# A frequency-mixing kernel: the last group of four takes other PSUM banks, and the edge columns are merged later

## The chip, the cores and the metric

The kernel runs on one core of a Trainium2 chip. The metric is the device time of one execution in microseconds (us), lower is better. The engines that matter are TensorE (PE in the profile; PEld is its weight load), VectorE (DVE), ScalarE (ACT), GpSimd (POOL) and SyncE (SP, which issues the large DMAs). Each has its own queue of instructions, works through it in order, and waits for the others by semaphores. PSUM, into which TensorE writes, has eight banks of 512 float32 for each of 128 partitions.

## The reference, cut to what matters

The input x is (4, 128, 128, 768) float32. The 768 channels are 8 blocks of 96, and each block has its own complex two-layer mixing.

```python
xf = jnp.fft.rfft2(x, axes=(1, 2), norm='ortho')            # (b, h, 65, c), then c -> 8 x 96
o1r = relu(einsum(xr, w1[0]) - einsum(xi, w1[1]) + b1[0])
o1i = relu(einsum(xi, w1[0]) + einsum(xr, w1[1]) + b1[1])
o2r = einsum(o1r, w2[0]) - einsum(o1i, w2[1]) + b2[0]
o2i = einsum(o1i, w2[0]) + einsum(o1r, w2[1]) + b2[1]
xc = softshrink(o2r, 0.01) + 1j * softshrink(o2i, 0.01)
return jnp.fft.irfft2(xc, s=(128, 128), axes=(1, 2), norm='ortho') + x
```

## The kernel before, in words

All transforms are matrix products with tables of cosines and sines. The work is cut into 32 steps (L23: `STEPS = B * NB // PAIRS` = 16 turns of a loop with two steps each), one for each pair of an image and a block of 96 channels. A step `q` has these stages.

1. Forward transform along one axis (`forward_lines`, L367): 26 groups of up to four channels. DVE or ACT packs each into `ring_a`, PE multiplies, and ACT or DVE moves the result from PSUM into `ydg`, an array of 128 columns (real and imaginary parts of the 65 frequencies kw) by 96 channels.
2. Mixing: the frequencies kw are worked through in 17 groups (`NU`; `GROUP_PAIRS`, L63), numbered u = 0 to 16. Groups 0 to 15 have four kw each, group 16 has one, kw = 1. Group 1 holds the edge columns kw = 0 and 64, and group 15 holds kw = 2 to 5. For each group PE does the transform along H (`fwd_big` L407, `fwd_small` L420), whose results are copied out of PSUM by ACT (`copy_big`, L567, into `zbig`) and DVE (`copy_small`, L668, into `zsmall`); PE does the first mixing layer (`mix1_whole`, `mix1_columns`, `mix1_rows`), ACT applies the relu (`relu`, L574: first `hsmall`, then `hbig`), PE does the second layer (`mix2_rows`, `mix2_whole`), and DVE adds the bias and applies the soft threshold (`shrink`, L675: three instructions of which the first, L691, reads PSUM, and the last, L701, writes `ydg`).
3. `merge` (L482) combines the edge columns by two matmuls, and ACT copies the result into columns 0 and 1 of `ydg` (L610).
4. Inverse transform along H (`inverse_lines`, L390): again 26 groups of up to four channels. The first six are packed into the ring `ring_h` in two parts: ACT takes columns 12 to 127 (L614), which need groups 0 to 14 of the mixing alone, and DVE takes columns 0 to 11 (L745), which need all groups and the merge. PE starts a group when both parts are there.
5. Inverse transform along W (`rows`, L488), with DVE and POOL adding the results onto the input, and SP storing them.

The order is written out by hand. PE's mixing loop has the groups staggered: in turn `it` PE transforms group `it`, does the first layer of group `it - 1` and the second of group `it - 2`. Behind the loop stand the second layer of group 15, the first of 16, the merge, and the second layer of 16.

The banks are: 0 the H transform's large part, 1 its small part, 2 and 3 the first layer's large part, 4 its small part, 5 and 6 the second layer's output, 7 the output of group 16 alone. The merge writes bank 1. Since all groups from 0 to 15 write their second layer to banks 5 and 6, `mix2_rows` waits until DVE has read the group before out of them (`bias_done`, which L691 raises):

```python
if 0 < u < NU - 1:
    pe.wait_ge(bias_done, NU * q + u)
```

In the mixing ACT's order for a turn is `copy_big(it)`, `relu(it - 1)`, and in turns 11 to 16 also one copy of the next step's input (L541); behind the loop it has the copy of the merge and the six packs. DVE's order is `copy_small(it)`, `shrink(it - 2)`, and in turns 4 to 10 some work on the next input.

Of the kernel before, what the change touches and what calls it, by code (L numbers as in the profile page):

```python
# [68 lines left out]
LATE = 12  # L69
# [107 lines left out]
def build(nc, x, mix, table, out):  # L177
    with ExitStack() as ctx:
# [76 lines left out]

        ZBIG_BANK, ZSMALL_BANK, BIG_BANK, SMALL_BANK, OUT_BANK, LAST_BANK = 0, 1, 2, 4, 5, 7
        E_BANK = ZSMALL_BANK
        ROW0_BANK = 2
# [48 lines left out]

        def out_bank(u):

            return LAST_BANK if u == NU - 1 else OUT_BANK  # L310

# [9 lines left out]
        with nc.Block() as block:  # L321
# [44 lines left out]
            def _(pe):  # L366
# [96 lines left out]
                def mix2_rows(q, u):  # L463
                    pe.wait_ge(hid_ready, NU * q + u + 1)
                    if 0 < u < NU - 1:
                        pe.wait_ge(bias_done, NU * q + u)
                    for k, pair in enumerate(GROUP_PAIRS[u]):
                        for i in range(2 if pair[1] is not None else 1):
                            half = slice(i * SMALL, (i + 1) * SMALL)
                            pe.matmul(ps[:, out_bank(u) + i, k * 2 * CB:(k + 1) * 2 * CB],  # L470
                                      hsmall[u % 2][half, k * H:(k + 1) * H],
                                      mix_part("w2_small")[half], start=k == 0, stop=False, skip_group_check=True)

                def mix2_whole(q, u):
                    n = len(evens(u))
                    for k in range(n + len(odds(u))):
                        o = ps[:, out_bank(u) + k // n, k % n * 2 * CB:(k % n + 1) * 2 * CB]
                        mm = pe.matmul(o, hbig[u % 2][:, k * H:(k + 1) * H], mix_part("w2_big"),  # L478
                                       start=False, stop=True, skip_group_check=True)
# [22 lines left out]
                with pe.Fori(0, STEPS) as t:  # L502
                    for p in range(PAIRS):
# [23 lines left out]
                        mix1_rows(q, NU - 1)  # L527
                        merge(q)
                        mix2_rows(q, NU - 1)
                        mix2_whole(q, NU - 1)  # L530
                        inverse_lines(q)
                        lines_moved(q, 1)
# [4 lines left out]
            def _(act):  # L537
# [21 lines left out]
                def move_row0(q):  # L559
# [4 lines left out]
                    act.dma_start(yedge[127:128, 0:4:2, :],  # L564
                                  row0[0:2]).then_inc(row0_moved, 16)

                def copy_big(q, u):  # L567
# [19 lines left out]
                def step(t, last):  # L587
                    for p in range(PAIRS):
# [11 lines left out]
                        for it in range(NU + 1):  # L600
                            if it < NU:
                                copy_big(q, it)
                            if it >= 1:
                                relu(q, it - 1)
                            if PACK_AT <= it < PACK_AT + RING_A and not (last and p == PAIRS - 1):

                                act.wait_ge(pairs_folded, FOLDS * (q + 2))
                                pack_lines(q + 1, 1 - p, it - PACK_AT)
                        act.wait_ge(merge_done, q + 1)
                        act.copy(ydg[:, 0:2, :].rearrange("p k c -> p (k c)"),  # L610
                                 ps[:, E_BANK, 0:2 * CB]).then_inc(merged, 1)
                        act.wait_ge(shrunk, NU * q + NU - 2)
                        for g in range(RING_H):
                            act.copy(*pack_moves(g, LATE, 128)).then_inc(packed_act, 1)  # L614
                        act.wait_ge(merged, q + 1)
# [12 lines left out]
            def _(dve):  # L628
# [46 lines left out]
                def shrink(q, u):  # L675
# [7 lines left out]

                    d = ps[:, out_bank(u):out_bank(u) + halves, 0:ne * 2 * CB].rearrange("p i (k c) -> p i k c", c=2 * CB)
                    b2 = mix_part("b2").rearrange("p (i k c) -> p i k c", i=1, k=1).broadcast_to([128, halves, ne, 2 * CB])
# [110 lines left out]
```

## Time and profile before

| | us |
|---|---|
| median of 3 runs | 5476.74 (5476.72 to 5477.54) |
| the profiled execution | 5478.67 |
| its span, from first to last instruction | 5475.4 |
| PE busy | 5302.9 (97%) |
| DVE busy | 3684.5 (67%) |
| ACT busy | 2217.8 (41%) |
| mean granted TensorE clock | 0.993 |

PE is busy nearly all the time, so the time is the sum of PE's work and of the short stretches in which it waits. [...] The profiled execution is 1.93 us longer than the median. In the chain of waits the profile puts 89% of the span to "issue", since it doesn't follow PE's busy time there; the chain is of no use here, and the waits and the timeline are read instead.

### The profile page before, as it was taken

Reading aid. Unit: us, or ns where it says so; the run is one execution under the profiler, and the core shown is the slowest. Engines: PE = TensorE matmul, PEld = TensorE weight load, DVE = VectorE, ACT = ScalarE, POOL = GpSimd, SP = SyncE. Lnnn points to the kernel's source line nnn. Section 1 sums busy time; section 2 is a strip of 40 time slices with the busy share of each in tenths; the row PEclk is TensorE's granted clock in tenths of the full one; section 3 lists DMA queues with packets and bytes.
Section 4 is the critical chain, followed back from the end, with each engine's and each line's share of the span. In section 5 each row is a group of like instructions: output and inputs, shape, how many; then the busy total and the mean of one; then the engine's idle time right before and its main releaser. Section 6 shows DMA issues by size and latency. Waiting matters only on the chain.

```text
span 5475.4 us, 112300 instructions
## 1 busy us (share of the span) xinstructions
PE 5302.9 (97%) x44352; PEld 4309.3 (79%) x44352; DVE 3684.5 (67%) x5859; ACT 2217.8 (41%) x3457; POOL 627.1 (11%) x420
## 2 busy tenths in 40 slices
PE   6999999999999999999999999999999999999998
PEld 5777887778777787777877777787778877787777
DVE  5676676676666766767667676676666766766665
ACT  3443434434344343444433443334434344343442
POOL 0110011110111101111011110011100111101111
PEclk9999999999999999999999999999999999999999
DMA  3331333312333113331133321333312333123311
GB/s 101 94 84 29 84 94 94 96 30 70 94 94 98 44 54 94 94 98 48 51 94 94 98 65 35 92 94 98 79 38 75 94 98 94 37 62 94 98 48 47
DMA packets 1065693, 421.12 MB, mean 77 GB/s; under 512 B 1062816, under 2 KB 1062944, under 8 KB 1065120
## 3 DMA queue, kind: packets, MB, share of 16 engines
q1 hardware_dynamic: 1060384, 411.62, 28.2%
q8 instruction: 391, 6.41, 0.5%
q10 hardware_dynamic: 4736, 1.60, 0.1%
q14 instruction: 182, 1.49, 0.1%
HBM read 210.26 MB, written 201.33 MB: 75 GB/s over the span
## 4 chain that ended last, share of the span: by engine, by line
issue 89%; POOL 11%; POOLq 0%; DVE 0%
POOL x L774 11%; POOLq L773 0%; POOLq L777 0%; DVE x L726 0%; POOLq L774 0%; POOLq L786 0%
## 5 line engine op out<-in xcount | busy, mean ns | idle before, releaser
L774 POOL TENSOR_TENSOR x<-shrink_or_v,x 128x480 f32<-128x480 f32 (+1 forms) x416 | 626.9, 1507 | 4840.6 <-DVE shrink_or_v L719 4800.9
L691 DVE TENSOR_TENSOR shrink_or_v<-ps,wts 128x768 f32<-128x768 f32 (+1 forms) x544 | 502.0, 923 | 993.1 <-PE ps L478 993.1
L478 PE MATMUL ps<-wts,hbig 128*128 128x192 f32 x4160 | 821.6, 340 | 0.0
L399 PE MATMUL ps<-tab,ring_h 128*128 128x128 f32 x6144 | 726.7, 283 | 46.2 <-DVE ring_h L745 46.2
L399 PEld LDWEIGHTS ps<-tab,ring_h 128*128 128x128 f32 x6144 | 720.6, 199 | 55.6 <-DVE ring_h L745 55.6
L478 PEld LDWEIGHTS ps<-wts,hbig 128*128 128x128 f32 x4160 | 661.0, 189 | 122.2 <-issue 122.2
L572 ACT COPY zbig<-ps 128x512 f32<-128x512 f32 (+1 forms) x544 | 309.1, 568 | 966.5 <-PE ps L415 966.5
L580 ACT ACTIVATE hsmall<-ps,wts 128x256 f32<-128x256 f32 (+1 forms) x544 | 254.6, 468 | 1084.8 <-PE ps L451 1084.8
L386 PE MATMUL ps<-tab,ring_a 128*64 128x128 f32 x6144 | 680.5, 273 | 3.8 <-ACT ring_a L541 3.8
L387 PE MATMUL ps<-tab,ring_a 128*63 128x128 f32 x6144 | 680.4, 273 | 0.0
L386 PEld LDWEIGHTS ps<-tab,ring_a 128*64 128x64 f32 x6144 | 671.3, 137 | 8.3 <-ACT ring_a L541 4.7
L387 PEld LDWEIGHTS ps<-tab,ring_a 128*63 128x63 f32 x6144 | 671.2, 136 | 0.0
L652 DVE COPY ydg<-ps 128x512 f32<-128x512 f32 (+5 forms) x768 | 504.0, 656 | 232.6 <-PE ps L399 149.9
L551 ACT COPY ydg<-ps 127x512 f32<-127x512 f32 (+5 forms) x896 | 503.0, 573 | 364.4 <-PE ps L399 195.6
L415 PE MATMUL ps<-tab,ydg 128*128 128x128 f32 x4032 | 549.6, 276 | 17.8 <-DVE ydg L652 17.8
L415 PEld LDWEIGHTS ps<-tab,ydg 128*128 128x128 f32 x4032 | 518.1, 191 | 36.0 <-issue 36.0
L442 PE MATMUL ps<-zbig,wts 128*128 128x256 f32 (+1 forms) x2112 | 540.0, 377 | 0.0
L701 DVE TENSOR_TENSOR ydg<-shrink_or_v 128x768 f32<-128x768 f32 (+2 forms) x544 | 489.1, 899 | 17.8
L541 ACT COPY ring_a<-x 128x508 f32<-128x508 f32 x448 | 479.6, 1072 | 9.8 <-PE ps L387 9.5
L470 PE MATMUL ps<-wts,hsmall 64*128 64x192 f32 x4160 | 440.3, 325 | 36.5 <-DVE shrink_or_v L691 36.5
L470 PEld LDWEIGHTS ps<-wts,hsmall 64*128 64x128 f32 x4160 | 372.3, 187 | 73.6 <-issue 52.2
L673 DVE COPY zsmall<-ps 128x256 f32<-128x256 f32 (+1 forms) x544 | 224.6, 413 | 289.3 <-PE ps L427 285.0
(52 smaller groups left out, 6620.3 us busy)
## 6 DMA issues: line engine op xcount, KB each, us to landing
x<-in_x SPq DMA_DIRECT2D x128, 1536.0 KB, 12.4
out<-x SPq DMA_DIRECT2D x352, 480.0 KB, 4.8
out<-x SPq DMA_DIRECT2D x32, 432.0 KB, 4.1
wts<-in_mix SPq DMA_DIRECT2D x16, 513.0 KB, 3.6
out<-x SPq DMA_DIRECT2D x32, 240.0 KB, 4.2
out<-x SPq DMA_DIRECT2D x32, 192.0 KB, 4.3
ydg<-row ACTq DMA_DIRECT2D x32, 48.0 KB
yedge<-row ACTq DMA_DIRECT2D x32, 0.8 KB
```

The costliest lines, as they stand in the source:

```text
L386: pe.matmul(o[0:HALF], slot[:, 0:HALF], mat("fwd_w"), start=True, stop=True)
L387: mm = pe.matmul(o[HALF:127], slot[:, HALF:127], mat("fwd_w_odd"), start=True, stop=True)
L399: mm = pe.matmul(ps[:, line_bank(1, g), j * 128:(j + 1) * 128], ring_h[g % RING_H][:, j, :], mat("inv_h"), start=True, stop=True)
L415: mm = pe.matmul(ps[:, ZBIG_BANK, k * H:(k + 1) * H], t[:, s:s + 2, :].rearrange("p k c -> p (k c)")[:, 0:BIG], mat("fwd_h"), start=True, ...
L442: pe.matmul(ps[:, BIG_BANK + i, 0:n], mix_part("w1_big")[:, 0:BIG], zbig[u % 2][:, a:b], start=True, stop=False)
L470: pe.matmul(ps[:, out_bank(u) + i, k * 2 * CB:(k + 1) * 2 * CB], hsmall[u % 2][half, k * H:(k + 1) * H], mix_part("w2_small")[half], start ...
L478: mm = pe.matmul(o, hbig[u % 2][:, k * H:(k + 1) * H], mix_part("w2_big"), start=False, stop=True, skip_group_check=True)
L551: act.copy(*line_moves(stage, g)).then_inc(line_act, 1)
L652: dve.tensor_copy(*line_moves(stage, g)).then_inc(line_dve, 1)
L691: dve.tensor_tensor(parts(v), d, b2, ALU.add).then_inc(bias_done, 1)
L701: dve.tensor_tensor(dst, parts(v)[:, :, first:ne, :], parts(c)[:, :, first:ne, :], ALU.subtract).then_inc(shrunk, 1)
L774: pool.tensor_tensor(xs[p][:, a:b, :], ucopy[g % 4][:, 0:b - a, :], mirror(xs[p], a, b), ALU.add).then_inc(plus_ready, 1)
```

## The change

Group 15 writes its second layer into banks 0 and 1 and no longer waits for `bias_done`; it waits for the last copies out of these banks instead (`zbig_ready`, `zsmall_ready`). Group 16 writes to bank 5 and waits until DVE has read group 14 from there. The merge has bank 7, and PE issues it behind the second layer of group 16. ACT issues the first of its six packs ahead of the relu of group 16, the second behind that relu and ahead of the copy of the merge, and the other four behind that copy; each pack now has its own wait for `shrunk` (groups 0 to 14).

```diff
--- before.py
+++ after.py
@@ -253,8 +253,7 @@
             a, b = MIX[name]
             return wts[:, a:b]
 
-        ZBIG_BANK, ZSMALL_BANK, BIG_BANK, SMALL_BANK, OUT_BANK, LAST_BANK = 0, 1, 2, 4, 5, 7
-        E_BANK = ZSMALL_BANK
+        ZBIG_BANK, ZSMALL_BANK, BIG_BANK, SMALL_BANK, OUT_BANK, E_BANK = 0, 1, 2, 4, 5, 7
         ROW0_BANK = 2
 
         def line_bank(stage, g):
@@ -305,9 +304,13 @@
 
             return (len(evens(u)) + len(odds(u))) * H
 
-        def out_bank(u):
-
-            return LAST_BANK if u == NU - 1 else OUT_BANK
+        def out_banks(u):
+
+            bank = ZBIG_BANK if u == NU - 2 else OUT_BANK
+            return slice(bank, bank + 2)
+
+        def out_bank(u, i):
+            return range(8)[out_banks(u)][i]
 
         def small_rows(u):
             return BIG if odds(u) else SMALL
@@ -462,19 +465,22 @@
 
                 def mix2_rows(q, u):
                     pe.wait_ge(hid_ready, NU * q + u + 1)
-                    if 0 < u < NU - 1:
-                        pe.wait_ge(bias_done, NU * q + u)
+                    if u == NU - 2:
+                        pe.wait_ge(zbig_ready, NU * (q + 1))
+                        pe.wait_ge(zsmall_ready, NU * (q + 1))
+                    elif u:
+                        pe.wait_ge(bias_done, NU * q + min(u, NU - 2))
                     for k, pair in enumerate(GROUP_PAIRS[u]):
                         for i in range(2 if pair[1] is not None else 1):
                             half = slice(i * SMALL, (i + 1) * SMALL)
-                            pe.matmul(ps[:, out_bank(u) + i, k * 2 * CB:(k + 1) * 2 * CB],
+                            pe.matmul(ps[:, out_bank(u, i), k * 2 * CB:(k + 1) * 2 * CB],
                                       hsmall[u % 2][half, k * H:(k + 1) * H],
                                       mix_part("w2_small")[half], start=k == 0, stop=False, skip_group_check=True)
 
                 def mix2_whole(q, u):
                     n = len(evens(u))
                     for k in range(n + len(odds(u))):
-                        o = ps[:, out_bank(u) + k // n, k % n * 2 * CB:(k % n + 1) * 2 * CB]
+                        o = ps[:, out_bank(u, k // n), k % n * 2 * CB:(k % n + 1) * 2 * CB]
                         mm = pe.matmul(o, hbig[u % 2][:, k * H:(k + 1) * H], mix_part("w2_big"),
                                        start=False, stop=True, skip_group_check=True)
                     mm.then_inc(mix2_done, 1)
@@ -525,9 +531,9 @@
                         mix1_whole(q, NU - 1)
                         mix1_columns(q, NU - 1)
                         mix1_rows(q, NU - 1)
-                        merge(q)
                         mix2_rows(q, NU - 1)
                         mix2_whole(q, NU - 1)
+                        merge(q)
                         inverse_lines(q)
                         lines_moved(q, 1)
                         for g in range(NF):
@@ -563,6 +569,11 @@
                     act.dma_start(ydg[127:128, :, :], row0[:]).then_inc(row0_moved, 16)
                     act.dma_start(yedge[127:128, 0:4:2, :],
                                   row0[0:2]).then_inc(row0_moved, 16)
+
+                def early_pack(q, g):
+
+                    act.wait_ge(shrunk, NU * q + NU - 2)
+                    act.copy(*pack_moves(g, LATE, 128)).then_inc(packed_act, 1)
 
                 def copy_big(q, u):
                     act.wait_ge(zbig_done, NU * q + u + 1)
@@ -600,18 +611,20 @@
                         for it in range(NU + 1):
                             if it < NU:
                                 copy_big(q, it)
+                            if it == NU:
+                                early_pack(q, 0)
                             if it >= 1:
                                 relu(q, it - 1)
                             if PACK_AT <= it < PACK_AT + RING_A and not (last and p == PAIRS - 1):
 
                                 act.wait_ge(pairs_folded, FOLDS * (q + 2))
                                 pack_lines(q + 1, 1 - p, it - PACK_AT)
+                        early_pack(q, 1)
                         act.wait_ge(merge_done, q + 1)
                         act.copy(ydg[:, 0:2, :].rearrange("p k c -> p (k c)"),
                                  ps[:, E_BANK, 0:2 * CB]).then_inc(merged, 1)
-                        act.wait_ge(shrunk, NU * q + NU - 2)
-                        for g in range(RING_H):
-                            act.copy(*pack_moves(g, LATE, 128)).then_inc(packed_act, 1)
+                        for g in range(2, RING_H):
+                            early_pack(q, g)
                         act.wait_ge(merged, q + 1)
                         act.wait_ge(shrunk, NU * q + NU)
                         lines(q, p, 1)
@@ -681,7 +694,7 @@
                     def parts(t):
                         return t.rearrange("p (i k c) -> p i k c", i=halves, c=2 * CB)
 
-                    d = ps[:, out_bank(u):out_bank(u) + halves, 0:ne * 2 * CB].rearrange("p i (k c) -> p i k c", c=2 * CB)
+                    d = ps[:, out_banks(u), 0:ne * 2 * CB][:, 0:halves].rearrange("p i (k c) -> p i k c", c=2 * CB)
                     b2 = mix_part("b2").rearrange("p (i k c) -> p i k c", i=1, k=1).broadcast_to([128, halves, ne, 2 * CB])
                     dve.wait_ge(mix2_done, NU * q + u + 1)
                     if u >= 2:
```

On PE, the end of the mixing in the first step of the loop. Before, from the second layer of group 15 on (L470 and L478 are the second layer, L442 to L459 the first layer of group 16, L485 and L486 the merge):

```order
L470 MATMUL ps<-wts,hsmall 128x192 [waits bias_done,hid_ready]
L470 MATMUL ps<-wts,hsmall 128x192 x3
L478 MATMUL ps<-wts,hbig 128x192 x4
L436 REGISTER_ALU
L442 MATMUL ps<-zbig,wts 128x128 [waits hid_ready,zsmall_ready,zbig_ready]
L445 MATMUL ps<-zsmall,wts 64x128
L451 MATMUL ps<-zbig,wts 64x128
L459 MATMUL ps<-zsmall,wts 128x128
L485 MATMUL ps<-edge,tab 128x192 [waits shrunk]
L486 MATMUL ps<-edge,tab 128x192
L470 MATMUL ps<-wts,hsmall 128x192 [waits hid_ready]
L478 MATMUL ps<-wts,hbig 128x192
```

In the changed kernel the same stretch (L476 and L484 are now the second layer, L445 to L462 the first layer of group 16, L491 the merge's first matmul):

```order
L469 REGISTER_ALU [waits hid_ready]
L476 MATMUL ps<-wts,hsmall 128x192 [waits zsmall_ready,zbig_ready]
L476 MATMUL ps<-wts,hsmall 128x192 x3
L484 MATMUL ps<-wts,hbig 128x192 x4
L439 REGISTER_ALU
L445 MATMUL ps<-zbig,wts 128x128 [waits hid_ready,zsmall_ready,zbig_ready]
L448 MATMUL ps<-zsmall,wts 64x128
L454 MATMUL ps<-zbig,wts 64x128
L462 MATMUL ps<-zsmall,wts 128x128
L476 MATMUL ps<-wts,hsmall 128x192 [waits bias_done,hid_ready]
L484 MATMUL ps<-wts,hbig 128x192
L491 MATMUL ps<-edge,tab 128x192 [waits shrunk]
```

The wait for `bias_done` has gone from group 15 to group 16, and the merge no longer stands between the first and the second layer of group 16.

On ACT, the same place. Before (L541 packs the next input, L580 and L583 are the relu, L610 the copy of the merge, L614 the packs):

```order
L541 COPY ring_a<-x 128x4x127 [waits pairs_folded]
L580 ACTIVATE hsmall<-ps,wts 64x128 [waits small_mixed,mix2_done]
L583 ACTIVATE hbig<-ps,wts 128x128 [waits big_mixed]
L610 COPY ydg<-ps 128x192 [waits merge_done]
L614 COPY ring_h<-ydg 128x4x116 [waits shrunk]
L614 COPY ring_h<-ydg 128x4x116 x5
```

In the changed kernel (L576 is the pack, L591 and L594 the relu, L624 the copy of the merge):

```order
L547 COPY ring_a<-x 128x4x127 [waits pairs_folded]
L576 COPY ring_h<-ydg 128x4x116 [waits shrunk]
L591 ACTIVATE hsmall<-ps,wts 64x128 [waits small_mixed,mix2_done]
L594 ACTIVATE hbig<-ps,wts 128x128 [waits big_mixed]
L576 COPY ring_h<-ydg 128x4x116 [waits shrunk]
L624 COPY ydg<-ps 128x192 [waits merge_done]
L576 COPY ring_h<-ydg 128x4x116 [waits shrunk] x4
```

Two of the six packs have moved ahead of the copy of the merge, and one of them ahead of the last relu. On DVE nothing moves.

## Rows read from the trace of the kernel before

**Rows 1.** Page, busy us, share of the span and number of instructions of each engine.

```profile
PE 5302.9 (97%) x44352; PEld 4309.3 (79%) x44352; DVE 3684.5 (67%) x5859; ACT 2217.8 (41%) x3457; POOL 627.1 (11%) x420
```

**Rows 2.** Waits of PE over the span: us in total, times, longest.

```profile
PE ps L399 <- DVE ring_h L745: 46.2, 32, 1.4
...
PE ps L470 <- DVE shrink_or_v L691: 36.5, 32, 1.1
```

**Rows 3.** Timeline, first step: start us, us, instruction, [idle before it]; groups 14 and 15.

```profile
158.88 0.28 DVE L673 COPY zsmall<-ps 64x128 f32<-64x128 f32 x1
...
159.37 0.69 ACT L583 ACTIVATE hbig<-ps,wts 128x512 f32<-128x512 f32 x1
159.91 1.57 PE L478 MATMUL ps<-wts,hbig 128*128 128x192 f32 x8
```

**Rows 4.** The same timeline, from DVE's reading of group 14 to PE's group 16.

```profile
161.51 0.96 DVE L691 TENSOR_TENSOR shrink_or_v<-ps,wts 128x768 f32<-128x768 f32 x1 [2.35 <-PE ps L478]
...
162.62 0.92 PE L470 MATMUL ps<-wts,hsmall 64*128 64x192 f32 x8 [1.14 <-DVE shrink_or_v L691]
163.10 0.96 DVE L701 TENSOR_TENSOR ydg<-shrink_or_v 128x768 f32<-128x768 f32 x1
...
164.87 0.38 PE L442 MATMUL ps<-zbig,wts 128*128 128x128 f32 x2
165.07 0.96 DVE L691 TENSOR_TENSOR shrink_or_v<-ps,wts 128x768 f32<-128x768 f32 x1 [1.01 <-PE ps L478]
...
165.91 0.49 PE L459 MATMUL ps<-zsmall,wts 64*128 64x128 f32 x2
```

**Rows 5.** The same timeline, from the last relu to the inverse transform.

```profile
166.07 0.36 ACT L580 ACTIVATE hsmall<-ps,wts 64x128 f32<-64x128 f32 x1 [5.05 <-PE ps L451]
...
166.32 0.59 PE L485 MATMUL ps<-edge,tab 128*128 128x192 f32 x2
166.43 0.37 ACT L583 ACTIVATE hbig<-ps,wts 128x128 f32<-128x128 f32 x1
...
167.17 0.59 PE L470 MATMUL ps<-wts,hsmall 64*128 64x192 f32 x2
167.28 0.32 ACT L610 COPY ydg<-ps 128x192 f32<-128x192 f32 x1 [0.48 <-PE ps L486]
167.49 5.49 ACT L614 COPY ring_h<-ydg 128x464 f32<-128x464 f32 x6
...
167.69 0.59 PE L478 MATMUL ps<-wts,hbig 128*128 128x192 f32 x2
168.32 0.36 DVE L691 TENSOR_TENSOR shrink_or_v<-ps,wts 128x192 f32<-128x192 f32 x1 [0.70 <-PE ps L478]
...
169.00 0.36 DVE L701 TENSOR_TENSOR ydg<-shrink_or_v 128x192 f32<-128x192 f32 x1
169.47 0.77 DVE L745 COPY ring_h<-ydg 128x48 f32<-128x48 f32 x6
...
169.72 5.02 PE L399 MATMUL ps<-tab,ring_h 128*128 128x128 f32 x28 [1.44 <-DVE ring_h L745]
```

**Rows 6.** Stretches behind the first L399 of four steps; the granted clock follows POOL.

```profile
170.70:172.60 1.90, 1.90 (x11) 1.90 (x10) 0.66 (x1) 1.90 (x3) 0.00 (x0) 0.50 0.00 0
340.60:342.50 1.90, 1.90 (x20) 1.90 (x19) 1.51 (x3) 1.90 (x3) 0.00 (x0) 1.00 0.80 253
...
849.00:850.90 1.90, 1.90 (x19) 1.90 (x19) 1.44 (x3) 1.90 (x3) 0.00 (x0) 1.00 0.00 0
...
5422.30:5424.20 1.90, 1.90 (x19) 1.90 (x19) 1.46 (x3) 1.90 (x3) 0.00 (x0) 1.00 0.00 0
```

**Rows 7.** Timeline, PE alone: the first L399 of the second, the fifth, the sixth step.

```profile
339.58 1.60 PE L399 MATMUL ps<-tab,ring_h 128*128 128x128 f32 x12 [1.44 <-DVE ring_h L745]
...
848.05 1.72 PE L399 MATMUL ps<-tab,ring_h 128*128 128x128 f32 x13 [1.44 <-DVE ring_h L745]
...
1016.28 1.46 PE L399 MATMUL ps<-tab,ring_h 128*128 128x128 f32 x6 [1.44 <-DVE ring_h L745]
```

## The prediction

> **What bounds the kernel now.** I read the page's first part first: PE is busy for 97% of the span and DVE, the next, for 67% [rows 1]. So PE's queue sets the time, and what counts is where PE stands idle and how fast it is clocked. The waits of PE over the span come second: apart from the wait for the first load, which comes once, the two largest are the one before L399, 46.2 us in 32 times, and the one before L470, 36.5 us in 32 times [rows 2]. Both come once in each of the 32 steps, 1.44 and 1.14 us long, and both stand at the end of the mixing, where the change is made. Third comes the timeline of that place in the first step [rows 3 to 5]. The reader should see there:
>
> - PE ends the second layer of group 14 at 161.48 (159.91 + 1.57) and starts that of group 15 at 162.62. In between DVE reads group 14 out of the banks (L691, 161.51 to 162.47) [rows 3, 4].
> - Behind it PE has work up to 168.28: second layer of 15, first of 16, merge, second of 16. Then DVE has a chain of its own: three instructions of `shrink` for group 16 (168.32 to 169.36), then L745 at 169.47, whose first copy lets L399 go at 169.72 [rows 5].
>
> Fourth comes the clock. In a stretch of 1.9 us behind the first L399 of each step, the granted clock is 0.50 in some steps and 1.00 in others. I asked for this stretch in all 32 steps: 20 show 0.50 and 12 show 1.00; [rows 6] has one of the first kind and three of the second. At 0.50 PE gets through 11 matmuls in the stretch, at 1.00 through 19 or 20. What such a fall costs can be read from the distance of the first L399 of neighbouring steps, both pairs from an even step to an odd one: behind a fall, 339.58 - 169.72 = 169.86 us; without one, 1016.28 - 848.05 = 168.23 us [rows 5, 7]. [...] All of them follow the idle of 1.44 us before L399, but the same idle brings a fall in one step and none in another, so the idle alone doesn't decide it.
>
> **The change, part by part.** I rebuild the first step from 161.48 on.
>
> *Group 15 in banks 0 and 1.* The wait for L691 is gone. The new waits are for the last copies out of the two banks: DVE's ended at 159.16, and ACT's stands in its queue ahead of the relu that ended at 160.06 [rows 3]. Both are long over at 161.48, so they cost nothing; the cover is 1.4 us. The second layer of 15 and the first of 16 start 1.14 us earlier: L442 at 163.73 instead of 164.87, and L459 ends at 165.26 (165.91 + 0.49 - 1.14) [rows 4]. Since a matmul can start before the one ahead of it has ended, it may be 0.1 more.
>
> *The first pack ahead of the last relu.* It waits for DVE's L701 of group 14, which ends at 164.06 [rows 4], and starts at about 164.11. Six packs take 5.49 us, 0.92 each [rows 5], so it ends at about 165.05. The relu of 16 could have started at 166.07 - 1.14 = 164.93. What is queued behind the waiting pack is just this relu, and PE waits for it: the price is 0.12 us. The two instructions of the relu take 0.73 us (166.07 to 166.80) [rows 5], so they end at 165.78. DVE's release of PE took 0.15 us (L691 ended at 162.47, L470 started at 162.62) [rows 4]; with 0.12 the second layer of 16 starts at 165.90, not at 167.17. PE idles some 0.64 us for it, in place of the merge that used to lie there. Its wait for `bias_done` of group 14 is over since 162.47 at the latest.
>
> *The end of group 16.* From its L470 to DVE's L691 it took 168.32 - 167.17 = 1.15 us [rows 5], so L691 starts at 167.05. DVE is free by then: its `shrink` of group 15 started at 165.07 behind an idle of 1.01 us [rows 4] and ended at 167.62 (168.32 less the idle of 0.70 [rows 5]). Now it starts right behind L701 at 164.08 and ends at 166.63. Group 16 then takes 1.04 us as before and is done at 168.09; with the same 0.11 us to L745 that is 168.20.
>
> *The merge behind it.* Its four matmuls took 0.85 us (166.32 to 167.17), and the second layer of 16 has two of one kind (0.52, from 167.17 to 167.69) and two like the merge's (0.43) [rows 5]. So the merge starts at 165.90 + 0.95 = 166.85. From its start to ACT's copy it took 0.96 us, and the copy 0.32 [rows 5]: 167.81 to 168.13. ACT is free: the second pack runs from about 165.8 to 166.75. DVE hears of the copy some 0.11 us later, at 168.24. So the merge, which was hidden before, now sets the end by a hair: L745 starts at 168.24 and L399, 0.25 us later as before, at 168.49. The gain is 169.72 - 168.49 = 1.23 us a step.
>
> The bounds: if no matmul of the merge overlaps the one ahead (its start at 167.01), the gain is 1.07; if matmuls close up at 161.48 and a release takes 0.05, it is 1.35. I take 1.23, for which each piece has a row. 32 x 1.23 = 39.4 us (34 to 43).
>
> *The other packs.* The four behind the copy of the merge start at 168.1 and end at about 171.9, where the sixth ended at 172.98 before. At full clock PE does 12 matmuls of the inverse transform in 1.60 us [rows 7], and a group has 8, so it takes about 1.0 us for one. It wants the third group at 170.4, when its pack has ended at 169.05, and the sixth at 173.3. The margin is 1.3 us; each pack checks a wait of its own now, but even a loss of 0.1 for each stays in it. ACT's first move of a result comes 1 us earlier, with PE 1.23 us earlier; PE needs that bank again only eight groups later. DMAs are neither added nor moved; SP's load of weights waits for the same `shrink` and goes with it.
>
> *The clock.* PE's idle at this place falls from 2.58 us a step to about 1.35 (0.64 and 0.75), and the longest piece from 1.44 to 0.75. That must change how often the clock falls, and the trace can't say by how much: before there was one long piece right before L399, now there are two short ones within 3.2 us, with matmuls on half the array between them. The ends are no fall at all (32.6 us gained) and a fall in each step (12 x 1.63 = 19.6 us lost). I take 10 falls, half of those before: the piece before L399 is about half as long, but a second piece of the same size now lies close ahead of it. That gives 10 x 1.63 = 16.3 us.
>
> **The sum.** 5478.67 - 39.4 - 16.3 = 5423.0 us against the profiled execution. That was 1.93 us over the median of the runs, so 5421 for the median.
>
> **The rivals.**
>
> *Falls as often as before, or in each step.* For it: the two short idles lie close together, and before, 1.44 us within a busy stretch was enough in 20 steps. Against it: each idle alone is far shorter. 20 falls give 5476.74 - 39.4 = 5437; 32 falls give 5457. [...] No trace here shows two short idles in a row with a fall.
>
> *The change doesn't reach L399.* If the relu of 16 came so late that its second layer started at 167.17 again, the two idles would only be merged into one: 5477. For it: a pack now stands ahead of that relu. Against it: the relu would have to start 1.3 us later than worked out.
>
> *Slower.* One mechanism: the first pack, at the head of ACT's queue, is held until DVE has finished group 15 and not just 14. Then it starts at 166.7, ends at 167.6, the relu ends at 168.33, the second layer of 16 starts at 168.45, and L399 comes at 171.04: 1.32 us later than before, 42 us in all, 5519; more with more falls. It decides from the point at which the relu starts after 166.28 (165.05 + 1.23). For it: the pack waits for a count of `shrunk`. Against it: the count is for groups 0 to 14, and DVE ends group 14 at 164.06, ahead of 15, in its own order.
>
> **Chances.** The forecast, with 0 to 20 falls, 0.74; its own range is 5401 to 5441. More than 20 falls 0.17. No effect at L399 0.04. Slower 0.03. Faster than my bounds allow 0.02. The range of 5402 to 5445 takes in the forecast and the nearer part of the first rival, and leaves out the others. A measurement of this kernel can tell about 0.2%, 11 us, from no change. 5457 is still below 5466, so faster by more than that has 0.74 + 0.17 + 0.02 = 0.93, the same 0.04, slower 0.03.
>
> **What would show it.** In the profile after: the wait of 36.5 us before group 15's second layer gone; a wait of PE for ACT's relu (`hsmall` or `hbig`) before group 16's second layer, 0.5 to 0.8 us in each step; the wait before the inverse transform's first matmul down from 1.44 to 0.6 to 0.9 us; ACT's first pack ending about 1 us behind L701 of group 14, and the last relu right behind it; a step of about 167.0 us where the clock stays at 1.00. The same stretches behind the first inverse matmul, and now also those ahead of it, tell how often the clock falls. The forecast is wrong if the sum of the two idles stays above 2 us a step, if another wait of PE has grown by what these have lost, or if the clock falls in more than 20 steps.

## The result, and the profile after

| | us |
|---|---|
| before, median of 4 runs | 5476.73 (5473.81 to 5477.54) |
| changed, median of 4 runs | 5411.15 (5408.80 to 5411.76) |
| ratio | 0.988, 95% interval 0.9863 to 0.9898 |
| changed, profiled execution | 5411.11, span 5408.8 |

The change makes the kernel 65.6 us faster, 1.2%. The forecast was 5421, with a range of 5402 to 5445.

The waits of PE over the span in the changed kernel (L402 is what L399 was, L476 what L470 was) answer to [rows 2]:

```profile
PE ps L402 <- DVE ring_h L758: 25.4, 32, 0.8
...
PE ps L476 <- ACT hbig L594: 15.7, 32, 0.5
```

The wait for DVE before group 15, 36.5 us, is gone. A wait of 0.49 us a step for ACT's relu has come before group 16's second layer, and the wait before the inverse transform has shrunk from 46.2 to 25.4 us. All other waits of PE are as before, within 1 us in all. The timeline of the first step answers to [rows 3 to 5]; this execution is 0.18 us behind the one before when it gets there (L484 of group 14 at 160.09 here, L478 at 159.91 there):

```profile
160.09 1.57 PE L484 MATMUL ps<-wts,hbig 128*128 128x192 f32 x8
...
161.59 0.92 PE L476 MATMUL ps<-wts,hsmall 64*128 64x192 f32 x8
...
163.28 0.96 DVE L714 TENSOR_TENSOR ydg<-shrink_or_v 128x768 f32<-128x768 f32 x1
...
164.28 1.01 ACT L576 COPY ring_h<-ydg 128x464 f32<-128x464 f32 x1 [3.06 <-DVE ydg L714]
...
164.88 0.49 PE L462 MATMUL ps<-zsmall,wts 64*128 64x128 f32 x2
...
165.18 0.37 ACT L591 ACTIVATE hsmall<-ps,wts 64x128 f32<-64x128 f32 x1
165.44 0.36 ACT L594 ACTIVATE hbig<-ps,wts 128x128 f32<-128x128 f32 x1
...
165.86 0.59 PE L476 MATMUL ps<-wts,hsmall 64*128 64x192 f32 x2 [0.49 <-ACT hbig L594]
...
166.81 0.49 PE L491 MATMUL ps<-edge,tab 128*128 128x192 f32 x2
...
167.66 0.32 ACT L624 COPY ydg<-ps 128x192 f32<-128x192 f32 x1 [0.92 <-PE ps L492]
167.69 0.36 DVE L714 TENSOR_TENSOR ydg<-shrink_or_v 128x192 f32<-128x192 f32 x1
...
168.15 0.78 DVE L758 COPY ring_h<-ydg 128x48 f32<-128x48 f32 x6
...
168.41 3.84 PE L402 MATMUL ps<-tab,ring_h 128*128 128x128 f32 x32 [0.80 <-DVE ring_h L758]
```

From group 14's second layer to the first inverse matmul it takes 168.41 - 160.09 = 8.32 us, where it took 169.72 - 159.91 = 9.81 us: 1.49 us less. DVE's last `shrink` ends at 168.05 and ACT's copy of the merge at 167.98, so the two ends are within 0.1 us, with DVE's own chain the later one.

The granted clock, a share of full speed, in a stretch of 1.9 us behind the first L402, for all 32 steps as in [rows 6], is 0.50 in 8 steps (20 before) and 1.00 in 24. A step with 0.50 is called a fall below. The first step, the first fall (fifth step) and the step behind it:

```profile
169.40:171.30 1.90, 1.90 (x19) 1.90 (x18) 1.47 (x3) 1.90 (x3) 0.00 (x0) 1.00 0.00 0
...
836.70:838.60 1.90, 1.90 (x11) 1.90 (x10) 0.66 (x1) 1.90 (x3) 0.00 (x0) 0.50 0.00 0
1005.10:1007.00 1.90, 1.90 (x19) 1.90 (x18) 1.47 (x3) 1.90 (x3) 0.00 (x0) 1.00 0.72 251
```

And the distance of neighbouring steps, from PE's timeline, for the pairs that [rows 7] has:

```profile
335.15 1.05 PE L402 MATMUL ps<-tab,ring_h 128*128 128x128 f32 x7 [0.80 <-DVE ring_h L758]
...
835.74 1.64 PE L402 MATMUL ps<-tab,ring_h 128*128 128x128 f32 x7 [0.80 <-DVE ring_h L758]
...
1004.11 1.16 PE L402 MATMUL ps<-tab,ring_h 128*128 128x128 f32 x8 [0.80 <-DVE ring_h L758]
```

At full clock an even step takes 335.15 - 168.41 = 166.74 us, against 168.23: 1.49 us less, as in the timeline. Behind a fall it takes 1004.11 - 835.74 = 168.37, so a fall still costs 1.63 us.

The gain is accounted for: 32 x 1.49 = 47.7 us from the waits and 12 falls fewer x 1.63 = 19.6 us from the clock, 67.3 of the 67.6 us between the two profiled executions (5478.67 and 5411.11). The two parts aren't of one kind: the experiments below show what brings the 47.7 us, and that the 19.6 us hang on how many steps the clock falls in, for which they find no rule.

### The profile page after: what moved, and what is told of

The parts are those of the page before. It is cut to its first block, busy times and chain, and to the rows that moved or that the text cites. A ratio compares the mean times of both kernels' runs of the same rounds, so it can differ in the third digit from the quotient of the medians.

```text
span 5408.8 us, 112364 instructions
## 1 busy us (share of the span) xinstructions
PE 5277.2 (98%) x44352; PEld 4290.2 (79%) x44352; DVE 3682.4 (68%) x5859; ACT 2216.0 (41%) x3457; POOL 626.8 (12%) x420
## 3 DMA queue, kind: packets, MB, share of 16 engines
q14 instruction: 182, 1.49, 0.1%
## 4 chain that ended last, share of the span: by engine, by line
issue 88%; POOL 11%; POOLq 0%; DVE 0%
POOL x L787 11%; POOLq L786 0%; POOLq L790 0%; DVE x L739 0%; POOLq L787 0%; POOLq L799 0%
## 5 line engine op out<-in xcount | busy, mean ns | idle before, releaser
L484 PE MATMUL ps<-wts,hbig 128*128 128x192 f32 x4160 | 821.6, 340 | 0.0
L484 PEld LDWEIGHTS ps<-wts,hbig 128*128 128x128 f32 x4160 | 661.0, 189 | 122.2 <-issue 122.2
L402 PE MATMUL ps<-tab,ring_h 128*128 128x128 f32 x6144 | 707.5, 279 | 25.4 <-DVE ring_h L758 25.4
L402 PEld LDWEIGHTS ps<-tab,ring_h 128*128 128x128 f32 x6144 | 701.4, 195 | 34.8 <-DVE ring_h L758 34.8
L583 ACT COPY zbig<-ps 128x512 f32<-128x512 f32 (+1 forms) x544 | 309.3, 569 | 966.4 <-PE ps L418 966.4
L591 ACT ACTIVATE hsmall<-ps,wts 128x256 f32<-128x256 f32 (+1 forms) x544 | 254.9, 469 | 921.9 <-PE ps L454 921.9
L445 PE MATMUL ps<-zbig,wts 128*128 128x256 f32 (+1 forms) x2112 | 540.0, 377 | 0.0
L714 DVE TENSOR_TENSOR ydg<-shrink_or_v 128x768 f32<-128x768 f32 (+2 forms) x544 | 489.1, 899 | 17.8
L476 PE MATMUL ps<-wts,hsmall 64*128 64x192 f32 x4160 | 440.3, 325 | 15.7 <-ACT hbig L594 15.7
L476 PEld LDWEIGHTS ps<-wts,hsmall 64*128 64x128 f32 x4160 | 371.4, 187 | 50.3 <-ACT hbig L594 21.8
```

The lines of the kernel that those rows point to most:

```text
L402: mm = pe.matmul(ps[:, line_bank(1, g), j * 128:(j + 1) * 128], ring_h[g % RING_H][:, j, :], mat("inv_h"), start=True, stop=True)
L445: pe.matmul(ps[:, BIG_BANK + i, 0:n], mix_part("w1_big")[:, 0:BIG], zbig[u % 2][:, a:b], start=True, stop=False)
L476: pe.matmul(ps[:, out_bank(u, i), k * 2 * CB:(k + 1) * 2 * CB], hsmall[u % 2][half, k * H:(k + 1) * H], mix_part("w2_small")[half], start= ...
L714: dve.tensor_tensor(dst, parts(v)[:, :, first:ne, :], parts(c)[:, :, first:ne, :], ALU.subtract).then_inc(shrunk, 1)
```

## The experiments

Eleven kernels ran. "Step" is the distance of the first inverse matmuls of an even step and the next, at full clock; "falls" is the number of steps with 0.50 in the stretch. Those two are read from the one profiled execution, so a number of falls is one count and not a mean. The kernel before ran beside all of them, with medians of 5475.76 to 5477.19.

| kernel | median, us | step, us | falls |
|---|---|---|---|
| before | 5476.73 | 168.23 | 20 |
| changed | 5411.15 | 166.74 | 8 |
| banks_only | 5410.82 | 167.02 | 3 |
| merge_only | 5471.66 | 168.55 | 10 |
| old_banks | 5457.21 | 168.07 | 10 |
| merge_ahead | 5414.18 | 167.02 | 2 |
| pack_behind | 5407.57 | 166.70 | 7 |
| before_filled | 5444.77 | 168.23 | 0 |
| after_filled | 5403.15 | 166.81 | 0 |
| banks_only_filled | 5406.77 | 167.02 | 0 |
| pack_behind_filled | 5395.59 | 166.70 | 0 |
| before_longer4 | 5519.51 | 169.12 | 30 |
| before_longer11 | 5535.45 | 170.69 | 6 |

(In before_longer4 only two even steps are at full clock, 169.12 and 169.13 us: the first inverse matmuls of the first pair start at 170.79 and 339.92. Its steps with a fall are mostly 170.6 to 170.7 us apart.)

### What each part is worth

**banks_only**: the kernel before with the change of banks and nothing else of the change. Its main lines are below; besides them the merge has bank 7, and `shrink` and `mix2_whole` take the banks from `out_banks`.

```diff
+        def out_banks(u):
+            bank = ZBIG_BANK if u == NU - 2 else OUT_BANK
+            return slice(bank, bank + 2)
...
-                    if 0 < u < NU - 1:
-                        pe.wait_ge(bias_done, NU * q + u)
+                    if u == NU - 2:
+                        pe.wait_ge(zbig_ready, NU * (q + 1))
+                        pe.wait_ge(zsmall_ready, NU * (q + 1))
+                    elif u:
+                        pe.wait_ge(bias_done, NU * q + min(u, NU - 2))
```

> The kernel before with the change of banks alone: group 15 in banks 0 and 1, group 16 in bank 5, the merge in bank 7 but still ahead of group 16's second layer, and ACT's order as before. Theory (the chain is first the wait before group 15, then first layer, merge, second layer and DVE's last chain): the first inverse matmul comes 1.21 us earlier in each step, so a step at full clock takes 168.23 - 1.21 = 167.02 us, the wait before L470 of group 15 is gone, the 1.44 us before L399 stays. With about 20 falls of the clock 5438 us; fewer falls would show that the 1.14 us before group 15 had a part in them. Rival (the banks bring little and the order of merge and packs brings the most): a step of 168 us and about 5470 us.

The step is 167.02 us, to the hundredth what was expected. The time isn't 5438 but 5410.82 us (ratio to before 0.9881, 0.9864 to 0.9897): the falls went from 20 to 3. Its timeline, where the idle before the inverse transform is the old one:

```profile
165.00 0.59 PE L491 MATMUL ps<-edge,tab 128*128 128x192 f32 x2
...
165.85 0.59 PE L476 MATMUL ps<-wts,hsmall 64*128 64x192 f32 x2
...
168.40 2.83 PE L402 MATMUL ps<-tab,ring_h 128*128 128x128 f32 x23 [1.44 <-DVE ring_h L751]
```

So one part of the change, in this measure, is as fast as the whole. The other parts shorten the step by 0.28 us more (9 us in all), and the falls give it back: a step behind a fall took 168.41 - 167.02 = 1.39 us more in banks_only, 4 us for 3 falls, against 8 x 1.63 = 13 us in the changed kernel.

**merge_only**: the kernel before with `merge(q)` behind group 16's second layer.

```diff
-                        merge(q)
                         mix2_rows(q, NU - 1)
                         mix2_whole(q, NU - 1)
+                        merge(q)
```

> The kernel before with the merge moved behind group 16's second layer, and nothing else: banks as before, ACT's packs all behind the copy of the merge. Theory: the second layer of group 16 starts 0.3 us earlier, but the copy of the merge ends 1.4 us later on ACT and the first pack ends behind it at 169.9 instead of 168.4, so that the first inverse matmul waits for ACT and comes 0.2 us later: a step at full clock of 168.4 us, about 5482 us at 20 falls. Rival (moving the merge is a gain by itself): 0.27 us a step earlier, 5468 us.

The step is 168.55, longer by 0.32 us, the theory's direction (it had 0.2). In its timeline DVE's part of the first group is there at about 170.0, and PE still waits for ACT's first pack, which could start only behind the copy of the merge:

```profile
169.38 0.32 ACT L610 COPY ydg<-ps 128x192 f32<-128x192 f32 x1 [1.85 <-PE ps L486]
...
169.60 1.89 ACT L614 COPY ring_h<-ydg 128x464 f32<-128x464 f32 x2
169.89 0.77 DVE L745 COPY ring_h<-ydg 128x48 f32<-128x48 f32 x6
...
170.72 0.48 PE L399 MATMUL ps<-tab,ring_h 128*128 128x128 f32 x2 [1.37 <-DVE ring_h L745]
```

(The view names DVE. Its six copies take 0.77 us from 169.89, so the first was done by about 170.0; the first of ACT's two packs, 1.89 us together from 169.60, ended at about 170.6. That it was the pack is worked out from these rows.) Yet the median is 5471.66 us (0.9997, 0.9987 to 1.0006), the same as before: the clock fell in 10 steps instead of 20, some 16 to 19 us less (a fall from an even step to the next costs only 1.3 to 1.6 us here), and this covers the 10 us that the longer steps cost. Its ten runs scatter from 5468.51 to 5485.86, more than those of any other kernel here.

**old_banks**: the changed kernel with group 15 in banks 5 and 6 and its wait for DVE, and group 16 in bank 0.

```diff
-            bank = ZBIG_BANK if u == NU - 2 else OUT_BANK
+            bank = ZBIG_BANK if u == NU - 1 else OUT_BANK
...
-                    if u == NU - 2:
+                    if u == NU - 1:
...
-                        pe.wait_ge(bias_done, NU * q + min(u, NU - 2))
+                        pe.wait_ge(bias_done, NU * q + u)
```

> The changed kernel with group 15's second layer back in banks 5 and 6 and its wait for DVE (group 16 takes bank 0 and the merge stays in bank 7, behind it, with the early packs). Theory: the 1.14 us before group 15 is back, part of it hidden as group 16's relu is then no longer held up: the first inverse matmul 0.35 us earlier than in the kernel before, a step at full clock of 167.9 us. Rival (the parts add up without overlap: 166.73 + 1.21): 167.94 us, which is the same, or the late merge delays DVE's last copies: 168.2 us or more.

The step is 168.07 us, 0.17 above the theory's 167.9 and below the 168.2 of a late merge: the parts add up almost, but not quite. The wait before group 15 is back (36.5 us), and PE waits 20.6 us for the relu and 25.4 us before the inverse transform. The banks are worth 168.07 - 166.74 = 1.33 us with the rest in place and 1.21 without, and the rest 0.16 without the banks and 0.28 with them.

**merge_ahead**: the changed kernel with `merge(q)` back ahead of group 16's second layer.

> The changed kernel with the merge ahead of group 16's second layer again, all else as changed. Theory (the early packs bring nothing without the later merge): the step at full clock of the banks alone, 167.02 us, the 0.49 us before the second layer of group 16 gone and 1.44 us before the inverse transform. Rival (the early packs bring something by themselves): below 166.9 us.

The step is 167.02 us, the theory's figure, and the waits are those of banks_only. The packs are worth nothing alone. Moved alone, the merge costs 0.32 us a step (merge_only), and with the packs it gains 0.16 (old_banks): they are what lets it move. The median of this kernel's two runs is 3 us above that of banks_only, because its steps over a turn of the loop take 0.5 us more than its even ones.

**pack_behind**: the changed kernel with both early packs behind group 16's relu.

```diff
-                            if it == NU:
-                                early_pack(q, 0)
                             if it >= 1:
                                 relu(q, it - 1)
...
+                        early_pack(q, 0)
                         early_pack(q, 1)
```

> The changed kernel with ACT's first pack behind group 16's relu, so that both early packs stand between that relu and the copy of the merge. Theory (the pack holds the relu up): the relu starts when PE's first layer of 16 lets it, 0.25 us earlier, PE's wait before the second layer of 16 falls from 0.49 to about 0.25 us, ACT is free just when the merge is done, and a step at full clock takes 166.73 - 0.25 = 166.48 us: 8 us less, before what the falls do. Rival (the relu isn't late, or the two packs in a row delay the copy of the merge): 166.7 us or more a step.

The theory fell: the step is 166.70, only 0.04 us less. The timeline says why:

```profile
164.80 0.48 PE L462 MATMUL ps<-zsmall,wts 64*128 64x128 f32 x2
164.97 0.36 ACT L591 ACTIVATE hsmall<-ps,wts 64x128 f32<-64x128 f32 x1 [3.85 <-PE ps L454]
...
165.32 0.37 ACT L594 ACTIVATE hbig<-ps,wts 128x128 f32<-128x128 f32 x1
165.59 1.93 ACT L576 COPY ring_h<-ydg 128x464 f32<-128x464 f32 x2
...
165.74 0.59 PE L476 MATMUL ps<-wts,hsmall 64*128 64x192 f32 x2 [0.46 <-ACT hbig L594]
```

The relu has two parts, and the second, L594, waits for the end of PE's L462 (165.28 here, 165.37 in the changed kernel) and starts 0.04 us behind it here, 0.07 there. The pack held the first part up, which the second's own wait hid.

### What the falls of the clock are worth, and what sets their number

The fillers are matmuls that multiply one table by another into a bank that is free at that point, and nothing reads them. In the profile each is two records.

```diff
+                def fill(n):
+                    for _ in range(n):
+                        pe.matmul(ps[:, BIG_BANK + 1, 0:H], mat("inv_h"), mat("fwd_h"), start=True, stop=True)
...
                         mix2_whole(q, NU - 1)
+                        fill(6)
                         inverse_lines(q)
```

**before_filled** (the edit shown):

> The kernel before with six matmuls more in each step, ahead of the inverse transform, in PE's idle of 1.44 us: they multiply two tables into a bank that is free then, and nothing reads them. Theory (20 falls to half the clock, 1.63 us each, come from the idle there): no falls in any step, the granted clock near 1.000, no work delayed, 5476.7 - 32.6 = 5444 us. Rival (the falls have another cause, or cost nothing since PE would wait anyway): 5477 us or a little more, with falls as before.

5444.77 us (0.9942, 0.9926 to 0.9959), within 1 us of the theory. The first step (L490 is the filler):

```profile
167.88 1.50 PE L490 MATMUL ps<-tab 128*128 128x128 f32 x12
169.49 2.27 PE L399 MATMUL ps<-tab,ring_h 128*128 128x128 f32 x18
...
170.50:172.40 1.90, 1.90 (x20) 1.90 (x19) 1.49 (x3) 1.90 (x3) 0.00 (x0) 1.00 0.00 0
```

The step stays 168.23, PE's wait before L399 is gone from the waits, and the clock is 1.00 in all 32 stretches. So the 20 falls cost 32 us, and the idle before the inverse transform is needed for them. The 1.14 us before group 15 are still there, 36.5 us in all, and bring no fall by themselves.

**after_filled** (two fillers behind `mix1_rows(q, NU - 1)`, three behind the merge), **pack_behind_filled** (three behind the merge in pack_behind) and **banks_only_filled** (six, in banks_only):

> The changed kernel with two such matmuls ahead of group 16's second layer (in the idle of 0.49 us) and three behind the merge (in the idle of 0.80 us). Theory: the 8 falls go, 8 x 1.63 = 13 us, 5398 us; a step of 166.73 us as at full clock before. Rival (the fillers delay the second layer of group 16 or the first inverse matmul by up to 0.1 us each): 5401 to 5404 us.

> The same with three matmuls more behind the merge, in PE's idle before the inverse transform. Theory: no falls, so the time follows from the step alone: 5403 us (the changed kernel filled) - 8 = 5395 us. Rival: falls remain, since the shorter idle before group 16's second layer isn't filled, and the time is 5400 us or more.

> The kernel with the change of banks alone, with six matmuls more in its idle of 1.44 us before the inverse transform. Its 3 falls go, so 5410.8 - 3 x 1.6 = 5406 us. Theory (the later merge with the early packs is worth 0.3 us a step, which the 8 falls of the changed kernel hide): this kernel stays 9 to 10 us slower than the changed kernel with the first pack behind the relu and its idle filled (5395.6 us). Rival (the later merge and the packs are worth nothing): 5396 us.

None of the three has a fall. after_filled is at 5403.15 us, as its rival had it: with the two fillers ahead of group 16's second layer, that layer starts 5.85 us behind L484 of group 14 and not 5.77, which makes a step 0.07 us longer, and its steps over a loop turn are mostly 167.2 to 167.4 us. pack_behind_filled is at 5395.59 (0.9852, 0.9835 to 0.9868), the fastest kernel of this study, 15.6 us below the changed one. banks_only_filled is at 5406.77, 11.2 us above it, so the theory holds: the later merge and the early packs are worth 0.3 us a step, which the falls hide in the changed kernel. The whole change, measured where neither kernel has a fall, is worth 5444.77 - 5403.15 = 41.6 us, and 49.2 us with the pack behind the relu (pack_behind_filled); the 65.6 us of the result hold falls besides.

**before_longer4 and before_longer11**: four and eleven fillers in turn 8 of the mixing, where PE has no gap. Here `fill` writes bank 7 (`LAST_BANK`), which in the mixing only group 16 uses.

```diff
                         for it in range(NU):
+                            if it == 8:
+                                fill(4)
                             fwd_big(q, it)
```

> The kernel before with four matmuls more in each step, in the middle of the mixing (turn 8), where PE is busy without a gap; they write a free bank, and nothing reads them. The idles stay as they are. In the trace before, the place of a fall relative to the first inverse matmul moves from step to step (0.28, then none, -0.46, 0.58 us and so on), and the kernel with the banks alone had 3 falls with the same idle of 1.44 us before that matmul. Theory (where the falls come out depends on the length of a step, and the idle only makes them possible): four matmuls of 0.215 us make a step 0.86 us longer, and the falls rise from 20 to 28 or more, so 5444.8 (no falls) + 27.5 + 28 x 1.6 = 5517 us or a little more. Rival (the wait of 1.14 us before group 15 took part, and its removal made the falls rare): falls stay at about 20, 5444.8 + 27.5 + 32.6 = 5505 us.

> The same with eleven matmuls, 2.37 us a step. Theory (length of the step): both idles are as before, yet the falls drop to 4 or fewer, 5444.8 + 75.7 + 4 x 1.6 = at most 5527 us, little more than with four matmuls. Rival (the idles set the number of falls): about 20 falls, 5444.8 + 75.7 + 32.6 = 5553 us.

The places of the falls that the first of the two names, in the trace before (first, second, third and fourth step; the granted clock follows POOL):

```profile
165.00:170.00 5.00, 3.56 (x19) 2.23 (x18) 3.99 (x11) 3.45 (x6) 0.00 (x0) 1.00 0.00 0
170.00:173.42 3.42, 3.42 (x18) 3.42 (x18) 1.00 (x5) 3.42 (x5) 0.00 (x0) 0.50 0.00 0
335.00:346.00 11.00, 9.56 (x72) 8.31 (x72) 8.60 (x19) 9.59 (x14) 0.00 (x0) 1.00 0.16 48
500.00:507.92 7.92, 5.80 (x33) 4.14 (x32) 5.82 (x9) 2.70 (x5) 0.00 (x0) 1.00 0.00 0
507.92:511.34 3.42, 2.95 (x14) 2.95 (x15) 1.56 (x8) 3.42 (x5) 0.00 (x0) 0.50 0.00 0
672.00:678.59 6.59, 5.15 (x29) 3.82 (x29) 4.58 (x13) 3.75 (x7) 0.00 (x0) 1.00 0.01 2
678.59:682.00 3.41, 3.41 (x19) 3.41 (x18) 1.33 (x3) 3.19 (x4) 0.00 (x0) 0.50 0.51 154
```

and the first L399 of the third and the fourth step:

```profile
508.39 0.58 PE L399 MATMUL ps<-tab,ring_h 128*128 128x128 f32 x1 [1.44 <-DVE ring_h L745]
...
678.01 0.38 PE L399 MATMUL ps<-tab,ring_h 128*128 128x128 f32 x1 [1.44 <-DVE ring_h L745]
```

So the clock falls 170.00 - 169.72 = 0.28 us behind the first L399 in the first step, not at all around the second's (339.58), 508.39 - 507.92 = 0.47 us ahead of it (0.46 before rounding) in the third and 678.59 - 678.01 = 0.58 us behind it in the fourth. The 28 and the 4 falls that the two theories name were the author's estimates; no run had shown them.

Both keep the waits of the kernel before: 46.1 us before L399 and 36.5 us before L470, 32 times each. With four fillers the clock falls in 30 steps (5519.51 us), with eleven in 6 (5535.45 us). Second and third step with four:

```profile
340.90:342.80 1.90, 1.90 (x11) 1.90 (x11) 0.66 (x1) 1.90 (x3) 0.00 (x0) 0.50 0.78 253
512.10:514.00 1.90, 1.90 (x11) 1.90 (x10) 0.66 (x1) 1.90 (x3) 0.00 (x0) 0.50 0.00 0
```

and with eleven:

```profile
346.60:348.50 1.90, 1.90 (x19) 1.90 (x18) 1.47 (x3) 1.90 (x3) 0.00 (x0) 1.00 0.70 251
517.70:519.60 1.90, 1.90 (x20) 1.90 (x19) 1.48 (x3) 1.90 (x3) 0.00 (x0) 1.00 0.00 0
```

The rival that takes the number of falls from the idles would have 20 in both. The same idles with more work in a busy place give 30 and 6. The theory's count of 4 for eleven was missed by two, and its time by 8 us: besides the two falls, a filler takes 0.22 us (169.12 - 168.23 = 0.89 for four, 170.69 - 168.23 = 2.46 for eleven) and not the 0.215 of the author's estimate, and over a loop turn a step takes 0.4 to 0.6 us more than an even step here. It isn't the distance from one step to the next as such that decides: from an even step it is about 170.7 us in most steps of both kernels, with a fall in nearly every step of one and in few of the other. And these runs don't say what made 20 falls into 3 in banks_only, where one idle went and the step became shorter at once.

## Why the prediction was right

*The bound and the place.* Right: the two waits of PE named there changed, the one forecast ahead of group 16 came (0.49 us, where 0.64 was forecast), and the others stayed.

*Group 15's banks.* Right. Forecast 1.14 us, "it may be 0.1 more"; group 15's second layer now starts 1.50 us behind the start of L484 of group 14, where it took 2.71, so 1.21 us; banks_only makes a step 1.21 us shorter.

*The first pack ahead of the relu.* The forecast's start of the relu, 5.14 us behind L478 of group 14 (165.05 - 159.91), was met (165.18 - 160.09 = 5.09). Its length was not: the 0.73 us of before hold a wait of the second part for PE. Both parts now take 0.62 us, the release of PE 0.06 instead of 0.12, and the second layer of 16 starts at 5.77, not 5.99. This is the mis-sized term, 0.22 of the 0.26 us a step by which the gain was forecast too low. Its cause, that the end of the relu hangs on PE's first layer and not on when ACT is free, is also why taking the pack away brought 0.04 us only; the price of 0.12 us for the pack was too high.

*The end.* Merge and `shrink` of 16 end within 0.1 us of each other, as forecast, with the order of the two reversed. L402 comes 8.32 us behind L484 of group 14 where 8.58 was forecast: the gain is 1.49 and not 1.23 us a step, 47.7 and not 39.4 us. It lies above the forecast's own bound of 1.35 as well, so the bounds were too narrow. That bound also counted an earlier group 15, although in the forecast's own chain the relu waits for the pack and DVE and gains nothing by it.

*The clock.* Its share was right in size and wrong in reason, and that it came near was luck. Forecast: 10 falls, 16.3 us, because the idle before L399 is half as long. Its 1.63 us for a fall are the difference of its two distances, 169.86 - 168.23, and the changed kernel has the same, 168.37 - 166.74. Measured: 8 falls, 12 fewer, 19.6 us. But banks_only has the full 1.44 us and 3 falls, and the kernel before has 6 or 30 with nothing changed but some matmuls in a busy place. Nor can one take the shorter idles as the cause of the 8: that wasn't tried apart from the length. What the runs show is that the idle must be there (no falls where it is filled) and that with the same idles the work in the rest of the step changes how many steps are hit; by what rule stays open. With the 0 to 30 falls that kernels here have, the same 47.7 us of waits would have given about 5396 to 5445 us (5476.73 - 47.7, less 20 x 1.63 or plus 10 x 1.63), so the forecast's range covered most of what the clock could do, and the trace before couldn't tell where in it the time would lie.

*The rivals.* Falls in each step didn't come about: the two short idles, 0.49 and 0.80 us, stand in all 32 steps, and the clock fell in 8 of them (in 20 of the 32 before). The case in which nothing reaches L399 is refuted by the 1.49 us, and the slower one, with the pack held until group 15, by the row of the pack, which starts at 164.28, 0.04 us behind the end of group 14's L714.

Against the profiled execution the forecast was 5423.0, and 5411.1 was measured: 8.3 us of the difference are waits and 3.3 us clock, and 0.3 us is left.

## What to carry to other kernels

Where PE works in equal steps and stands idle for a short time in each, look at the granted clock behind the idle in every step, not at its mean: 0.993 looked harmless and hid 32 us. A few matmuls that nobody reads, placed in the idle, took that back; with six of them in an idle of 1.44 us the step kept its length, with two in one of 0.49 us it became 0.07 us longer. They also make two versions comparable: without them, a step 0.3 us shorter or longer could change the number of falls by more than the edit was worth (merge_only: 0.32 us a step longer, 10 us in all, and 10 falls fewer, 16 to 19 us), so judge an edit by the length of a step at full clock beside the total. And before pricing an instruction that is put ahead of another, look at what each part of the other one waits for.

## What the runs showed of the hardware

- The number of falls changes strongly when matmuls are added where PE is busy and the idles stay: 20 falls with steps of 168.23 us at full clock, 30 at 169.12, 6 at 170.69 and, with one idle fewer, 3 at 167.02. With the idle before the inverse transform filled there is none, though the idle of 1.14 us before group 15 stays (before_filled).
- A fall from an even step to the next costs 1.63 us in most steps of the kernel before (8 of 10; 1.40 and 1.49 in the others) and in both such steps of the changed one, 1.39 us in the one of banks_only, and 1.3 to 1.6 us in merge_only.
- An even step at full clock repeats within 0.04 us inside one kernel. A step over the loop's turn doesn't: from nothing to 0.6 us more, in some kernels nearly always (merge_ahead, 167.4 to 167.6 against 167.02), in others seldom. These are up to about 7 us of a kernel's time; their cause stays open.
